# Digits of sorted positions moved from VectorE to GpSimd, and their squares from GpSimd to ScalarE, in a fused attention and mixture-of-experts kernel

## The chip, the cores and the metric

The kernel runs on one core of a Trainium2 chip. A core has five engines that run their own instruction streams in order and meet at semaphores: TensorE (PE in the profile), VectorE (DVE), ScalarE (ACT), GpSimd (POOL) and SyncE (SP, which here only starts DMAs). The metric is the time on the device in microseconds (us); the kernel before takes 2859.86 us, the median of three runs.

## What is computed

Images are cut into 36 patches of 16 x 16 and embedded to 192 numbers each, 77 text tokens are appended, and the 16 x 113 = 1808 tokens go through one attention layer and then through a feed-forward part with a shared expert and 16 gated experts. The gated experts are what matters here. For each token `x` (192 numbers) and each expert `i`:

```
gate_feature = hidden_states * pe[i] @ gate_w + gate_b      # 192 numbers
gate_weight, gate_idx = top_k(gate_feature, 96)             # sorted, with positions
gate_weight = softmax(gate_weight)
gathered = take_along_axis(hidden_states, gate_idx, axis=-1)
y = y + (silu((gathered * gate_weight) @ eg_w[i]) * ((gathered * gate_weight) @ eu_w[i])) @ ed_w[i]
```

So every token needs, for every expert, the 96 largest of 192 gate features in order, their positions, and the token's own numbers at those positions. The positions run from 0 to 191. The softmax subtracts the largest value, which is the first of the sorted ones.

## The kernel before, in words

**Tiles and blocks.** Behind the attention part (the first 335 us or so) the 1808 tokens are worked in 14 tiles of 128 tokens and one rest of 16 tokens, which is packed into one tile's width. A tile's 16 experts are four groups of four; one group of one tile is a block. The rest is block 0 (two packed bands in place of four experts), and the tiles are blocks 1 to 56. `slot(t, g, mlp)` is what each engine does for group `g` of tile `t`; the loop over `t` is unrolled by four groups.

**The search, on VectorE (`slot`, lines 850 to 885).** For each block VectorE handles two pairs of experts. Per pair there are 12 rounds; a round finds the 8 largest (`max`, L867), their positions (`max_index`, L871) and strikes them out (`match_replace`, L873) for both experts of the pair. After the first round of the next block `close_block` (L837) closes the block before: it writes the negated maxima `ntop` (L842) and splits the 384 positions of the block into a high digit (position / 16, L846) and a low digit (position mod 16, L847), both as 16-bit integers in `digits`, and raises `ranked`. VectorE runs ahead of the other engines: for block n it waits only for the gate features of that block and for the softmax weights of block n-2.

**The gather, on the four others.** The gather is made of matmuls. The digits of block n+1 are turned to bf16 by ScalarE (`prepare`, L918) and squared by GpSimd (`square`, L1096); digits and squares (`dcode`) go by DMA to HBM and back into `rows`, laid out anew. In the slot of block n each engine goes through 16 steps (octs, `o` = 0 to 15). Per oct TensorE builds a one-hot code (`make_code`, L1190), ScalarE takes it out of PSUM (`code_out`, L935), TensorE looks the tokens up with it (`look`, L1205), ScalarE takes the result out (L946), GpSimd multiplies it with the second half of the code (`picked`, L1110), and TensorE places the product (`put`, L1214). TensorE builds the code of oct o+2 while it looks up oct o, and has only one PSUM buffer for it: code o+2 waits until ScalarE has taken out code o+1. Between the octs stand the experts' matmuls of the block before (`up` L1252, `down` L1269), ScalarE's `activate` and GpSimd's `hide` for them, and the gate matmuls of the next tile (L1171).

**Where the two halves meet.** `PREPARE` is 8: behind oct 8 of the slot of block n, ScalarE does `prepare(n + 1)`, for which it waits for `ranked`, and GpSimd does `square(n + 1)` behind its `picked` of oct 8, for which it waits for ScalarE's `plain`. Everything on these two engines that is written behind these points waits with them, the four `exponentials` of block n+1 (octs 9 to 12) and all the code and look work of octs 9 to 15 included.

Of the kernel before, what the change touches and what calls it, by code (L numbers as in the profile page):

```python
# [25 lines left out]
TOP = D // 2  # L26
# [548 lines left out]
PREPARE = 8  # L575

# [23 lines left out]
def experts(nc, sb, sem, tok_d, norm_d, normt_d, digit_d, out, ident, wgate, gatew, pe_col, rows, table, wshared, wsdown, wexp, wdown,  # L600
# [11 lines left out]
    digits = sb("digits", [TILE, 2, 2, COLS], U16)  # L612
# [39 lines left out]
    plain = sem("plain")  # L652
# [21 lines left out]
    def steady(eng):  # L674

        eng.sem_inc(passed, 1)
# [67 lines left out]
    with nc.Block() as block:  # L744
# [79 lines left out]
        def _(dve):  # L824
# [12 lines left out]
            def close_block(n, par):  # L837

                many = experts_of(n)
                last = 1 if many > 2 else 0  # L840
                dve.wait_ge(chains[last], LAST_STEP)
                nc.vector.tensor_scalar(ntop[:, par, 0:many], vals[:, par, 0:many, 0], -1.0, None, ALU.mult)  # L842
                if not (isinstance(n, int) and n < 2):
                    dve.wait_ge(plain, n - 1)
                src = idx[:, par, 0:many].rearrange("p e r -> p (e r)")
                nc.vector.tensor_scalar(digits[:, par, 0, 0:many * TOP], src, 4, None, ALU.logical_shift_right)  # L846
                nc.vector.tensor_scalar(digits[:, par, 1, 0:many * TOP], src, LO - 1, None, ALU.bitwise_and).then_inc(ranked, 1)  # L847
                dve.sem_clear(chains[last])

            def slot(t, g, mlp):  # L850
# [3 lines left out]
                for pair in range(many // 2):  # L854
# [26 lines left out]
                    found.then_inc(chain, 1)  # L881
                    done += 1
                    assert done == LAST_STEP
# [15 lines left out]
        def _(act):  # L899
# [12 lines left out]
            def prepare(n, par):  # L912
                act.wait_ge(ranked, n + 1)

                if not isinstance(n, int) or n >= 2:
                    act.wait_ge(digits_out, 16 * n - 16)
                w = experts_of(n) * TOP
                nc.scalar.activation(dcode[:, par, :, 1, 0:w], digits[:, par, :, 0:w], ACT.Copy).then_inc(plain, 1)  # L918
# [128 lines left out]
        def _(pool):  # L1047
# [44 lines left out]
            def square(n, par):  # L1092

                pool.wait_ge(plain, n + 1)
                w = slice(0, experts_of(n) * TOP)
                nc.gpsimd.tensor_tensor(dcode[:, par, :, 0, w], dcode[:, par, :, 1, w], dcode[:, par, :, 1, w],  # L1096
                                        ALU.mult).then_inc(coded, 1)

            def slot(t, g, mlp):
# [5 lines left out]
                for o in range(OCT):  # L1105
# [6 lines left out]
                    if o == PREPARE and not last_block(n):  # L1112
                        square(n + 1, 1 - par)
# [45 lines left out]
            square(0, 0)  # L1159
# [263 lines left out]
```

## Time and profile before

| | |
|---|---|
| median of three runs | 2859.86 us (2857.23 to 2862.73) |
| the profiled execution | 2860.59 us, of which its span is 2858.9 us |
| busy: DVE | 2572.4 us, 90% of the span |
| busy: PE | 2389.7 us, 84% |
| busy: ACT | 1679.0 us, 59% |
| busy: POOL | 1657.0 us, 58% |
| mean granted TensorE clock | 0.929 |

A busy time is the sum of an engine's own instructions; an engine that waits for a semaphore isn't busy. In the row views the last bracket of a row is the idle time of that engine just before the instruction, and what ended it.

### The profile page before, as it was taken

To read this page: it belongs to the slowest core of one execution; us is meant where nothing else is said; L and a number is where in the kernel's file an instruction comes from. 1 tells how busy PE (TensorE), PEld (TensorE's weight loads), DVE (VectorE), ACT (ScalarE), POOL (GpSimd) and SP (SyncE) were. 2 spreads that over 40 slices of the span, in tenths; PEclk is the share of its full clock that TensorE was granted. 3 is DMA by queue.
4 is the path that set the end of the run, shared out by engine and by line. 5 is a ranking of instruction groups with operands and counts; after the bars stand their busy time and mean duration, and the time that the engine had idled before them with its cause. 6 is when DMAs were issued, how large, how long until landed. Compare 5 with 4: busy or idle time off the path is not lost.

```text
span 2858.9 us, 55365 instructions
## 1 busy us (share of the span) xinstructions
PE 2389.7 (84%) x12314; PEld 1572.6 (55%) x12314; DVE 2572.4 (90%) x13628; ACT 1679.0 (59%) x3895; POOL 1657.0 (58%) x2118
## 2 busy tenths in 40 slices
PE   4999649998888887888888888888888888888887
PEld 3677426655555554555555555555555555555554
DVE  2454499999999999999999999999999999999980
ACT  1343233776656666666666656666666666666664
POOL 0110023776766676675666766666676666667675
PEclk9898668999999999999999999999999999999998
DMA  3000410110110111110110110111110110110110
GB/s 97 25 25 24 119 23 14 26 28 15 31 24 17 28 25 21 25 28 16 28 28 14 32 25 16 28 25 21 25 28 16 29 28 14 32 25 15 25 23 5
DMA packets 159240, 77.93 MB, mean 27 GB/s; under 512 B 105911, under 2 KB 156204, under 8 KB 156876
## 3 DMA queue, kind: packets, MB, share of 16 engines
q1 hardware_dynamic: 158156, 72.39, 12.5%
q8 instruction: 127, 2.08, 0.3%
q14 instruction: 253, 2.07, 0.2%
q0 software_dynamic: 704, 1.39, 0.1%
HBM read 39.04 MB, written 27.77 MB: 23 GB/s over the span
## 4 chain that ended last, share of the span: by engine, by line
DVE 85%; PE 2%; issue 1%; ACT 1%; POOL 0%; DMA 0%; POOLq 0%; DVEq 0%; ACTq 0%
DVE idx L871 30%; DVE keys L873 29%; DVE vals L867 24%; DVE digits L847 0%; PE ps L1252 0%; DVE digits L846 0%; PE ps L1214 0%; PE ps L1269 0%; DVE keys_rest L873 0%; PE ps L1190 0%; ACT code L935 0%; DVE ntop L842 0%; PE ps L1205 0%; ACT gu_s L977 0%; PE ps L1181 0%
## 5 line engine op out<-in xcount | busy, mean ns | idle before, releaser
L871 DVE FIND_INDEX8 idx<-vals,keys 128x8 uint16<-128x192 f32 x2688 | 1234.6, 465 | 0.0
L873 DVE MATCH_REPLACE8 keys<-vals,keys 128x192 f32<-128x192 f32 x2464 | 1124.7, 456 | 0.0
L867 DVE MAX8 vals<-keys 128x8 f32<-128x192 f32 x2688 | 973.2, 461 | 0.0
L1110 POOL TENSOR_TENSOR picked<-looked_s,code 128x384 f32<-128x384 f32 (+1 forms) x912 | 810.1, 904 | 76.8 <-ACT looked_s L946 68.1
L935 ACT ACTIVATE code<-ps 128x768 bf16<-128x768 f32 (+1 forms) x912 | 735.6, 807 | 187.2 <-PE ps L1190 168.3
L1190 PE MATMUL ps<-rows,codew 128*128 128x384 bf16 (+1 forms) x1824 | 469.8, 340 | 355.9 <-ACT code L935 326.0
L1214 PE MATMUL ps<-picked,place 128*128 128x384 f32 (+1 forms) x1824 | 753.0, 501 | 0.0
L1205 PE MATMUL ps<-code,table 128*128 128x384 bf16 (+1 forms) x2736 | 615.2, 335 | 29.7 <-issue 29.7
L946 ACT ACTIVATE looked_s<-ps 128x384 f32<-128x384 f32 (+1 forms) x912 | 445.6, 489 | 125.9 <-PE ps L1205 122.9
L871 DVE MATCH_VALUE_LOAD idx<-vals,keys 128x8 f32 x2688 | 512.6, 191 | 0.0
L1190 PEld LDWEIGHTS ps<-rows,codew 128*128 128x128 bf16 x1824 | 150.1, 99 | 575.8 <-ACT code L935 487.7
L873 DVE MATCH_VALUE_LOAD keys<-vals,keys 128x8 f32 x2464 | 456.6, 185 | 0.0
L1205 PEld LDWEIGHTS ps<-code,table 128*128 128x128 bf16 x2736 | 273.9, 101 | 274.2 <-issue 144.4
L1214 PEld LDWEIGHTS ps<-picked,place 128*128 128x128 f32 x1824 | 335.8, 198 | 77.3 <-issue 8.3
L1075 POOL TENSOR_TENSOR prod_s<-gu_s 96x256 f32<-96x256 f32 (+1 forms) x256 | 184.6, 721 | 304.6 <-ACT gu_s L977 301.0
L1252 PEld LDWEIGHTS ps<-xwt,wexp 96*96 96x96 f32 x1792 | 232.8, 171 | 35.2 <-issue 21.3
L1252 PE MATMUL ps<-xwt,wexp 96*96 96x128 f32 x1792 | 246.0, 283 | 1.6 <-ACT gu_s L977 1.0
L1096 POOL TENSOR_TENSOR dcode<-dcode 128x768 bf16<-128x768 bf16 (+1 forms) x57 | 82.9, 1454 | 264.7 <-ACT dcode L918 264.7
L918 ACT ACTIVATE dcode<-digits 128x768 bf16<-128x768 uint16 (+1 forms) x57 | 47.7, 837 | 281.2 <-DVE digits L847 281.2
L976 ACT ACTIVATE tanh_s<-ps 96x256 f32<-96x256 f32 x254 | 95.7, 377 | 193.5 <-PE ps L1252 152.2
L1269 PEld LDWEIGHTS ps<-wdown,hid 96*128 96x128 f32 (+1 forms) x960 | 165.4, 185 | 67.1 <-POOL hid L1079 7.2
L1269 PE MATMUL ps<-wdown,hid 96*128 96x192 f32 (+1 forms) x960 | 195.7, 328 | 2.8 <-POOL hid L1079 2.8
(139 smaller groups left out, 2557.9 us busy)
## 6 DMA issues: line engine op xcount, KB each, us to landing
digit_d<-dcode SPq DMA_DIRECT2D x56, 384.0 KB, 2.6
rows<-digit_d SPq DMA_DIRECT2D x112, 192.0 KB, 4.7
table<-parts SPq DMA_DIRECT2D x240, 9.0 KB
rows<-fill SPq DMA_DIRECT2D x1, 3072.0 KB
wexp<-in_w_exp SPq DMA_DIRECT2D x1, 2304.0 KB
wdown<-in_w_down SPq DMA_DIRECT2D x1, 2304.0 KB
hr<-norm_d SPq DMA_DIRECT2D x120, 12.0 KB
patch<-in_patches SPq DMA_DIRECT2D x16, 108.0 KB, 2.0
```

Source lines behind the costliest of these rows:

```text
L867: nc.vector.max(vals[:, par, e, at], from_keys[:, e, :]).then_inc(chain, 1)
L871: found = nc.vector.max_index(idx[:, par, e, at], vals[:, par, e, at], from_keys[:, e, :])
L873: nc.vector.match_replace(from_keys[:, e, :], vals[:, par, e, at], from_keys[:, e, :], NEG).then_inc(chain, 1)
L935: nc.scalar.activation(code[:, o % 4, :, 0:w], ps[:, CODE_B:CODE_B + 2, 0:w], ACT.Relu).then_inc(code_ready, 1)
L946: nc.scalar.activation(looked_s[:, o % 4, 0:w], ps[:, LOOK_B + o % 2, 0:w], ACT.Copy).then_inc(looked_out, 1)
L1075: nc.gpsimd.tensor_tensor(prod_s[:, u % 2, :, w], gu_s[:, u % 2, 0, :, w], gu_s[:, u % 2, 1, :, w], ALU.mult).then_inc(half_hidden, 1)
L1110: nc.gpsimd.tensor_tensor(picked[:, o % 4, w], looked_s[:, o % 4, w], code[:, o % 4, 1, w], ALU.mult).then_inc(picked_ready, 1)
L1190: ins = nc.tensor.matmul(ps[:, CODE_B + a, w], codew[:, a, :], rows[:, par, o, w], start=True, stop=True)
L1205: ins = nc.tensor.matmul(ps[:, LOOK_B + o % 2, w], table[:, o, s, :], code[:, o % 4, 0, w], start=(s == 0), stop=(s == 2))
L1214: nc.tensor.matmul(ps[:, XG_B, w], place[:, OCT - 1 - o:OCT - 1 - o + TILE], picked[:, o % 4, w], start=(o == 0), stop=(o == OCT - 1)).the ...
L1252: ins = nc.tensor.matmul(dst, wexp[:, e, at:at + HALF], xwt[:, e % GRP, :], start=True, stop=True)
L1269: ins = nc.tensor.matmul(ps[0:REST if rest else TILE, Y_B, 0:D], hid[:, u % 2, c, own], w, start=(u == 0 and c == 0), stop=(u == last_u an ...
```

## The change

VectorE no longer closes a block with three instructions. The last `max_index` of a block raises `ranked` by itself, and `close_block` only waits for the chain semaphore and clears it. GpSimd gets `part_ranks` in the place of `square`: behind `picked` of oct 8 it waits for `ranked` and for the digits' DMA of two blocks before, then writes `ntop`, and makes the digits in fp32. `rough` is position - 7.5 plus a large constant (1.5 x 2^27), at whose size fp32 has steps of 16, so that the sum is rounded to a multiple of 16; `whole` is the position as fp32; `high` is `rough` less the constant; the high digit is that over 16, and the low digit is `whole` less `high`. Both digits are written to `dcode` as bf16, and `parted` is raised. ScalarE's `prepare` waits for `parted` in place of `ranked` and squares the digits (`Square`) in place of copying them, and raises `coded` for the DMA. The semaphore `plain` and VectorE's wait for it are gone; `snapped` orders the steps within `part_ranks`.

```diff
--- before.py
+++ after.py
@@ -573,6 +573,7 @@
 TURN = 2
 DOWN_LAG = 3
 PREPARE = 8
+SNAP = 1.5 * 2.0 ** 27
 
 REST_LIST = [(0, None, 0), (1, None, 1), (2, "band", 0), (3, "band", 1)]
 assert len(REST_LIST) == REST_UNITS
@@ -609,7 +610,9 @@
     keys_rest = sb("keys_rest", [TILE, BANDS, D])
     vals = sb("vals", [TILE, 2, GRP, TOP])
     idx = sb("idx", [TILE, 2, GRP, TOP], U16)
-    digits = sb("digits", [TILE, 2, 2, COLS], U16)
+    rough = sb("rough", [TILE, COLS])
+    whole = sb("whole", [TILE, COLS])
+    high = sb("high", [TILE, COLS])
     dcode = sb("dcode", [TILE, 2, 2, 2, COLS], BF16)
     codew = sb("codew", [128, 2, 128], BF16)
     code = sb("code", [TILE, 4, 2, COLS], BF16)
@@ -649,7 +652,7 @@
     b_ones, b_codew = sem("b_ones"), sem("b_codew")
     gated, keys_ready = sem("gated"), sem("keys_ready")
     chains = sem("chain_first"), sem("chain_second")
-    plain = sem("plain")
+    parted, snapped = sem("parted"), sem("snapped")
     ranked, coded, digits_out, rows_in = sem("ranked"), sem("coded"), sem("digits_out"), sem("rows_in")
     inverted = sem("inverted")
     weights_ready = sem("weights_ready")
@@ -838,13 +841,7 @@
 
                 many = experts_of(n)
                 last = 1 if many > 2 else 0
-                dve.wait_ge(chains[last], LAST_STEP)
-                nc.vector.tensor_scalar(ntop[:, par, 0:many], vals[:, par, 0:many, 0], -1.0, None, ALU.mult)
-                if not (isinstance(n, int) and n < 2):
-                    dve.wait_ge(plain, n - 1)
-                src = idx[:, par, 0:many].rearrange("p e r -> p (e r)")
-                nc.vector.tensor_scalar(digits[:, par, 0, 0:many * TOP], src, 4, None, ALU.logical_shift_right)
-                nc.vector.tensor_scalar(digits[:, par, 1, 0:many * TOP], src, LO - 1, None, ALU.bitwise_and).then_inc(ranked, 1)
+                dve.wait_ge(chains[last], LAST_STEP - 1)
                 dve.sem_clear(chains[last])
 
             def slot(t, g, mlp):
@@ -878,9 +875,11 @@
                             close_pair(0)
                         if r == 0 and pair == 0 and not (isinstance(n, int) and n < 2):
                             close_block(n - 1, 1 - par)
-                    found.then_inc(chain, 1)
-                    done += 1
-                    assert done == LAST_STEP
+                    assert done == LAST_STEP - 1
+                    if pair == many // 2 - 1:
+                        found.then_inc(ranked, 1)
+                    else:
+                        found.then_inc(chain, 1)
                 if last_block(n) or is_rest(t):
                     close_block(n, par)
 
@@ -910,12 +909,12 @@
                                      ACT.Copy).then_inc(xwt_ready, 1)
 
             def prepare(n, par):
-                act.wait_ge(ranked, n + 1)
+                act.wait_ge(parted, n + 1)
 
                 if not isinstance(n, int) or n >= 2:
                     act.wait_ge(digits_out, 16 * n - 16)
                 w = experts_of(n) * TOP
-                nc.scalar.activation(dcode[:, par, :, 1, 0:w], digits[:, par, :, 0:w], ACT.Copy).then_inc(plain, 1)
+                nc.scalar.activation(dcode[:, par, :, 0, 0:w], dcode[:, par, :, 1, 0:w], ACT.Square).then_inc(coded, 1)
 
             def exponentials(n, par, e):
 
@@ -1089,12 +1088,24 @@
                         bass.AP(tensor=p_ap.tensor, offset=p_ap.offset, ap=[list(p_ap.ap[0]), [1, EXPERTS], [0, REST]]),
                         ALU.mult).then_inc(packed, 1)
 
-            def square(n, par):
-
-                pool.wait_ge(plain, n + 1)
-                w = slice(0, experts_of(n) * TOP)
-                nc.gpsimd.tensor_tensor(dcode[:, par, :, 0, w], dcode[:, par, :, 1, w], dcode[:, par, :, 1, w],
-                                        ALU.mult).then_inc(coded, 1)
+            def part_ranks(n, par):
+
+                many = experts_of(n)
+                pool.wait_ge(ranked, n + 1)
+                if not isinstance(n, int) or n >= 2:
+                    pool.wait_ge(digits_out, 16 * n - 16)
+                steady(pool)
+                src = idx[:, par, 0:many].rearrange("p e r -> p (e r)")
+                w = slice(0, many * TOP)
+                nc.gpsimd.tensor_scalar(ntop[:, par, 0:many], vals[:, par, 0:many, 0], -1.0, 0.0, ALU.mult, ALU.add)
+                nc.gpsimd.tensor_scalar(rough[:, w], src, 0.5 - LO / 2, SNAP, ALU.add, ALU.add).then_inc(snapped, 1)
+                nc.gpsimd.tensor_scalar(whole[:, w], src, 1.0, 0.0, ALU.mult, ALU.add).then_inc(snapped, 1)
+                pool.wait_ge(snapped, 4 * n + 1)
+                steady(pool)
+                nc.gpsimd.tensor_scalar(high[:, w], rough[:, w], SNAP, 0.0, ALU.subtract, ALU.add).then_inc(snapped, 1)
+                nc.gpsimd.tensor_scalar(dcode[:, par, 0, 1, w], rough[:, w], SNAP, 1.0 / LO, ALU.subtract, ALU.mult).then_inc(snapped, 1)
+                pool.wait_ge(snapped, 4 * n + 4)
+                nc.gpsimd.tensor_tensor(dcode[:, par, 1, 1, w], whole[:, w], high[:, w], ALU.subtract).then_inc(parted, 1)
 
             def slot(t, g, mlp):
                 n, par = block_no(t, g), parity(t, g)
@@ -1110,7 +1121,7 @@
                     nc.gpsimd.tensor_tensor(picked[:, o % 4, w], looked_s[:, o % 4, w], code[:, o % 4, 1, w],
                                             ALU.mult).then_inc(picked_ready, 1)
                     if o == PREPARE and not last_block(n):
-                        square(n + 1, 1 - par)
+                        part_ranks(n + 1, 1 - par)
                     for (u, e, half), spot in zip(units, spots):
                         if spot == o:
                             hide(tm, u, e)
@@ -1156,7 +1167,7 @@
             pack()
             for step in range(4):
                 split_part(0, step)
-            square(0, 0)
+            part_ranks(0, 0)
             slots(pool, slot)
             for u, e, half in units_of(BPT - 1):
                 hide(TILES, u, e)
```

VectorE, the end of the first full block and the first round of the next, before (`chain_second` is the second pair's semaphore, ISA the semaphore's clearing):

```order
L871 MAX_INDEX idx<-vals,keys 128x8 [waits chain_first]
L873 MATCH_REPLACE keys<-vals,keys 128x192
L871 MAX_INDEX idx<-vals,keys 128x8 [waits chain_first]
L873 MATCH_REPLACE keys<-vals,keys 128x192
L842 TENSOR_SCALAR ntop<-vals 128x4 [waits chain_second]
L846 TENSOR_SCALAR digits<-idx 128x384
L847 TENSOR_SCALAR digits<-idx 128x384
L848 ISA
L867 MAX vals<-keys 128x8 [waits chain_first] x2
```

and in the changed kernel:

```order
L868 MAX_INDEX idx<-vals,keys 128x8 [waits chain_first]
L870 MATCH_REPLACE keys<-vals,keys 128x192
L868 MAX_INDEX idx<-vals,keys 128x8 [waits chain_first]
L870 MATCH_REPLACE keys<-vals,keys 128x192
L845 ISA [waits chain_second]
L864 MAX vals<-keys 128x8 [waits chain_first] x2
```

Three instructions between the first round's last `match_replace` and the next round's `max` are gone; the clearing stays.

GpSimd, in the tiles' loop around oct 8 of one slot (split of the token table, then `picked`, then the prepare step), before:

```order
L1066 TENSOR_TENSOR parts<-rest,parts 96x16x16 [waits rounded]
L1106 REGISTER_ALU
L1110 TENSOR_TENSOR picked<-looked_s,code 128x384 [waits placed,looked_out]
L1094 REGISTER_ALU
L1096 TENSOR_TENSOR dcode<-dcode 128x2x384 [waits plain]
L1106 REGISTER_ALU
L1110 TENSOR_TENSOR picked<-looked_s,code 128x384 [waits placed,looked_out]
L1071 REGISTER_ALU
```

and in the changed kernel:

```order
L1117 REGISTER_ALU
L1121 TENSOR_TENSOR picked<-looked_s,code 128x384 [waits placed,looked_out]
L1094 REGISTER_ALU
L1096 ISA [waits ranked]
L1100 TENSOR_SCALAR ntop<-vals 128x4 [waits digits_out]
L1101 TENSOR_SCALAR rough<-idx 128x384
L1102 TENSOR_SCALAR whole<-idx 128x384
L1103 ISA
L1105 TENSOR_SCALAR high<-rough 128x384 [waits snapped]
L1106 TENSOR_SCALAR dcode<-rough 128x384
L1107 REGISTER_ALU
L1108 TENSOR_TENSOR dcode<-whole,high 128x384 [waits snapped]
L1117 REGISTER_ALU
L1121 TENSOR_TENSOR picked<-looked_s,code 128x384 [waits placed,looked_out]
```

In the place of one instruction that waited for `plain` there are six, of which the first waits for `ranked`, and two wait for GpSimd's own results. ScalarE's order is as it was, with the wait for `parted` in the place of that for `ranked`, and SyncE's order is the same.

## Rows read from the trace of the kernel before

**Rows 1.** The page's chain that ended last, shares of the span by engine.
```profile
DVE 85%; PE 2%; issue 1%; ACT 1%; POOL 0%; DMA 0%; POOLq 0%; DVEq 0%; ACTq 0%
```

**Rows 2.** Timeline, closing of one block: start us, us, engine, line, operation, tiles [idle].
```profile
2041.47 0.47 DVE L871 FIND_INDEX8 idx<-vals,keys 128x8 uint16<-128x192 f32 x1
...
2043.30 0.47 DVE L873 MATCH_REPLACE8 keys<-vals,keys 128x192 f32<-128x192 f32 x1
2043.56 0.28 DVE L842 TENSOR_SCALAR ntop<-vals 128x4 f32<-128x4 f32 x1
...
2043.96 0.74 DVE L867 MAX8 vals<-keys 128x8 f32<-128x192 f32 x2
2044.29 0.84 ACT L918 ACTIVATE dcode<-digits 128x768 bf16<-128x768 uint16 x1 [4.21 <-DVE digits L847]
```

**Rows 3.** Timeline, the closings of blocks 9 and 49, and GpSimd beside one.
```profile
753.20 0.67 POOL L1066 TENSOR_TENSOR parts<-rest,parts 96x256 bf16<-96x256 f32 x1
...
753.27 0.62 DVE L842 TENSOR_SCALAR ntop<-vals 128x4 f32<-128x4 f32 x1
...
754.86 0.61 DVE L867 MAX8 vals<-keys 128x8 f32<-128x192 f32 x2
...
2473.33 0.62 DVE L842 TENSOR_SCALAR ntop<-vals 128x4 f32<-128x4 f32 x1
...
2474.93 0.61 DVE L867 MAX8 vals<-keys 128x8 f32<-128x192 f32 x2
```

**Rows 4.** Timeline, ScalarE and GpSimd at the prepare steps of blocks 2, 3, 56.
```profile
452.68 0.84 ACT L918 ACTIVATE dcode<-digits 128x768 bf16<-128x768 uint16 x1 [13.18 <-DVE digits L847]
...
509.72 0.84 ACT L918 ACTIVATE dcode<-digits 128x768 bf16<-128x768 uint16 x1
...
511.02 1.46 POOL L1096 TENSOR_TENSOR dcode<-dcode 128x768 bf16<-128x768 bf16 x1
...
2773.12 0.47 DVE L871 FIND_INDEX8 idx<-vals,keys 128x8 uint16<-128x192 f32 x1
...
2774.16 0.84 ACT L918 ACTIVATE dcode<-digits 128x768 bf16<-128x768 uint16 x1 [4.21 <-DVE digits L847]
```

**Rows 5.** Groups by line, GpSimd, 512 to 2776 us: xcount | busy, mean ns | idle before.
```profile
L1096 POOL TENSOR_TENSOR dcode<-dcode 128x768 bf16<-128x768 bf16 x54 | 79.1, 1466 | 206.4 <-ACT dcode L918 206.4
```

**Rows 6.** Timeline, one prepare step in a slot with a long wait.
```profile
1313.72 0.84 ACT L918 ACTIVATE dcode<-digits 128x768 bf16<-128x768 uint16 x1 [8.42 <-DVE digits L847]
...
1314.64 1.47 POOL L1096 TENSOR_TENSOR dcode<-dcode 128x768 bf16<-128x768 bf16 x1 [7.68 <-ACT dcode L918]
```

**Rows 7.** Groups by line and form, GpSimd, whole span.
```profile
L1110 POOL TENSOR_TENSOR picked<-looked_s,code 128x384 f32<-128x384 f32 x896 | 801.4, 910 | 58.4 <-ACT looked_s L946 56.1
...
L1063 POOL CAST parts<-rest 96x256 bf16<-96x256 f32 x15 | 6.2, 416 | 0.2 <-POOL rest L1059 0.2
...
L313 POOL COPY hkept<-h 113x192 f32<-113x192 f32 x16 | 5.5, 345 | 1.2 <-DVE xn L401 1.2
L1135 POOL TENSOR_SCALAR st<-st 128x1 f32<-128x1 f32 x15 | 2.9, 190 | 1.9 <-ACT ysq L1003 0.8
```

**Rows 8.** Waits: who waited for whom, us in total, times, longest.
```profile
ACT code L935 <- POOL picked L1110: 11.2, 15, 0.8
...
PEld ps L1269 <- POOL hid L1079: 7.2, 17, 1.8
```

**Rows 9.** Timeline, ScalarE's wait and TensorE's beside it, a short wait.
```profile
1227.77 0.84 ACT L918 ACTIVATE dcode<-digits 128x768 bf16<-128x768 uint16 x1 [2.34 <-DVE digits L847]
...
1229.75 0.50 PE L1190 MATMUL ps<-rows,codew 128*128 128x384 bf16 x2 [0.17 <-ACT code L935]
```

**Rows 10.** Windows: busy us (x) of PE, PEld, DVE, ACT, POOL, then PEclk, DMA.
```profile
1312.00:1319.00 7.00, 3.30 (x10) 1.78 (x11) 7.00 (x41) 4.65 (x12) 4.20 (x5) 0.53 0.18 59
```

**Rows 11.** Groups by line, ScalarE, whole span.
```profile
L1003 ACT ACTIVATE ysq<-y,st 128x192 f32<-128x192 f32 x15 | 6.8, 455 | 9.5 <-POOL st L1131 9.5
...
L320 ACT ACT_TABLE_LOAD x1 | 1.3, 1283 | 0.9 <-PEq L1413 0.9
```

## The prediction, on record before the changed kernel ran

> **What bounds the kernel now.** Read the chain that ended last first: 85% of the span is VectorE [rows 1], and in the expert part VectorE never idles, since every row of a block's closing starts on the heels of the one before [rows 2]. Then ask who waits for VectorE. ScalarE does at the prepare step (2.3 to 13.2 us in the rows shown, [rows 2, 4, 6, 9]), and GpSimd, which stands behind ScalarE there, waits 206.4 us in 53 blocks, 3.89 us a block [rows 5]. So the gathering half has room, but only 3.89 us of 43, and the question of this change is whether what is put onto GpSimd still fits in it. That is read from two pitches.
>
> VectorE's pitch: the closing of block 39 starts at 2043.56 and that of block 49 at 2473.33 [rows 2, 3], which is 42.98 us a block.
>
> The gather's own pitch, if VectorE were never late: from block 3's ScalarE step (509.72) to block 56's (2774.16) there are 53 blocks in 2264.44 us [rows 4]. Less the 206.4 us that GpSimd waited, 2058.0 remain, 38.83 a block. That runs from GpSimd's square to its arrival at the next prepare step. ScalarE starts its own step 0.92 us before that square (1313.72 against 1314.64, [rows 6]), so from ScalarE's resuming to GpSimd's next arrival it is 39.75 us. GpSimd arrives later than ScalarE: at block 3 nobody waited for VectorE, ScalarE was there at 509.72 and GpSimd at 511.02, behind its `picked` of oct 8 [rows 4]. In row pair 6 the same gap is 8.42 + 0.92 - 7.68 = 1.66.
>
> **The change part by part.** *VectorE.* The three instructions that go cost less than their own durations (0.28 us for `ntop` alone), because they overlap: from `ntop` to the next `max` it is 2043.96 - 2043.56 = 0.40 us [rows 2]. 55 full closings lie inside the stream: 22.0 us (block 0's short one is left out). Twice the same stretch took 754.86 - 753.27 = 1.59 and 2474.93 - 2473.33 = 1.60 us [rows 3], 2.4 us more together, each time with GpSimd at work at the start. Together 24.4 us, and VectorE's pitch becomes 42.98 - 0.40 = 42.58. The semaphore's clearing stays; it stood beside the searches and costs nothing as long as they are issued ahead.
>
> On those two slow closings: `ntop` started 0.07 us after a GpSimd instruction. The Trainium skill, "SBUF — State Buffer", section "Who interferes with whom", says that a VectorE tensor_scalar can take the second port pair, which GpSimd shares, and that whoever is first keeps it for the whole instruction. The trace agrees, with these 1.2 us; by that rule they end with the change, and the searches, which run at 0.26 us steps whatever GpSimd does, don't feel GpSimd's added work.
>
> *GpSimd.* Away goes the square of 768 elements, 1.466 us a block [rows 5]. It stood behind ScalarE, so nothing but the digits' DMA and GpSimd's next `picked` waited for it. In come six instructions. A tensor_scalar of one element costs 0.190 [rows 7], so `ntop` 0.19. The trace has no long tensor_scalar on GpSimd. The nearest are the other one-input operations: a copy of 192 elements 0.345, a cast of 256 0.416 [rows 7]. Over the 0.190 that is 0.81 to 0.89 ns an element; 384 elements give 0.50 to 0.53. From above the bound is the two-input product of 384 elements, 0.910 [rows 7]; from below 0.345, the copy of half the size. I take 0.50, nearest to the one-input rows. Four of them 2.0; the last, with two inputs, 0.90; 0.08 us each for the wait on its own results and for the handing over to ScalarE (as 1314.64 follows 1313.72 + 0.84, [rows 6]): 0.19 + 2.0 + 0.90 + 0.16 = 3.25 us a block. With the bounds it is 2.6 and 4.9.
>
> The skill's "GPSIMD Engine Reference", section 4.1 "Engine selection", says that GpSimd is about twice as slow as VectorE with two inputs and roughly at line rate with one. By that rule the four cost 0.5 each and the sum is the same; it speaks against the upper bound.
>
> *ScalarE.* The square of 768 bf16 elements takes the place of a copy of the same size, 0.84 [rows 2]: nothing. Squares run already on ScalarE without a second table load [rows 11]; were one needed at each, it would be 2 x 1.3 us a block.
>
> *The new wait.* Before, ScalarE's step needed only VectorE, and GpSimd squared beside ScalarE's next octs. Now ScalarE stands from its arrival until GpSimd has arrived and worked 3.25 us. Behind it on ScalarE are the looks' and codes' evictions of octs 9 to 15; TensorE can't build code 12 before code 11 is taken out, so it stops too. The gather's pitch becomes 39.75 + 3.25 = 43.00 us, against VectorE's 42.58: the gather is now the slower half. As VectorE isn't held back, all of it shows at the end.
>
> **The sum.** Block 2's step still waits for VectorE (13.18 us before, [rows 4]). Its start moves by: 3.25 us behind the last `max_index`'s end in place of 2044.29 - (2041.47 + 0.47) = 2.35 [rows 2], +0.9; two closings less, -0.7: +0.2. GpSimd comes to block 3 at 511.02 + 0.2 = 511.2, ScalarE resumes at 514.5. Block 56: 514.5 + 53 x 43.00 = 2793.5, against 2774.16: +19.3 us. From there on the tail is as before. Off goes what GpSimd's relief gives: it is free when ScalarE resumes, where before it was busy until 2.39 us after. All that anyone waited for it in those places was 11.2 and 7.2 us [rows 8]; between 0 and 18.4 I take 5. So +14.3 us on the profiled 2860.6: 2874.9. The median of the runs lies 0.7 below the profiled execution: 2874.
>
> **The rivals.**
> (A) VectorE stays the bound, and the change is faster. Mechanism: TensorE works ahead while ScalarE stands, so that a stall isn't paid in full. For it: a stall of 2.34 us of ScalarE left TensorE idle for only 0.17 us [rows 9]. Against it: 39.75 was measured between a resuming behind such a stall and the next arrival, so what TensorE had done ahead is in it already. Time: -24.4, and at the end +2.7, since the last step starts 3.25 us behind the last search's end and not at 2774.16 - (2773.12 + 0.47) = 0.57 [rows 4]: -21.7, 2838. It decides fully where a block's stall adds under 2.6 us in place of 3.25; at 2.98 the time is that of before.
> (B) GpSimd's fp32 tensor_scalar on 16-bit positions runs at the two-input rate, 0.91. Then 4 x 0.41 = 1.64 more in each of 54 steps: 88.6 us, 2963. For it: two arithmetic steps and a conversion in each. Against: the casts convert at 0.416 for 256.
> (C) No change: both effects cancel. It is the strip between the forecast and A, a stall of 2.9 to 3.1 us.
> A further cost in either direction is TensorE's clock. The window behind and around the end of a long stall shows a granted clock of 0.53 of full speed [rows 10], that is mostly the lower of its two levels, 1.2 in place of 2.4 GHz. The new stalls are shorter than the longest of before but come in every slot; I leave it at nothing, give or take 10 us.
>
> **Chances and range.** The forecast, gather-bound at one-input rates, 0.55, with its own range 2850 to 2900 (0.45 to 0.60 us for an instruction moves it by -11 and +22, the relief by +5 and -13). A in whole or part 0.25, of which 0.03 ends within the strip. B or something between it and the forecast 0.20. What a measurement of this kernel can tell from no change is 0.2%, 5.7 us. Faster: 0.22 + 0.01 = 0.23; same: 0.03 + 0.09 = 0.12; slower: 0.45 + 0.20 = 0.65. The range leaves a tenth out on each side: from 2843, within A, to 2950, short of B's end.
>
> **What would show it.** In the profile after: GpSimd's four long tensor_scalars near 0.50 us; `max` following the first round's last `match_replace` at 0.26; almost no idle time of GpSimd before `ntop` from block 3 on, ScalarE idle some 4 to 5 us before its square and waiting for GpSimd, not for VectorE; squares at a pitch of 43.0; and VectorE done with the last block at about 2749, some 40 us before GpSimd comes for it. If GpSimd still waits for `max_index` at most prepare steps and the last one follows VectorE at once, A holds. If the tensor_scalars read 0.8 or more, B.

## The result, and the profile of the changed kernel

The changed kernel takes 3082.0 us, median of 4 runs (3081.7 to 3085.5); the kernel before, on the same chip, 2858.6 (2857.0 to 2862.7). The ratio is 1.078, 95% interval 1.076 to 1.080: 223 us slower. The forecast was 2874, its range ended at 2950. The sign was right, the size was not.

The page of the changed kernel (span 3080.0 us): busy times, the granted clock in 40 slices, and the chain that ended last.
```profile
PE 2433.7 (79%) x12314; PEld 1590.7 (52%) x12314; DVE 2551.3 (83%) x13457; ACT 1684.1 (55%) x3895; POOL 1930.3 (63%) x2403
...
PEclk9999578998898999988999999989889899899998
...
PE 33%; POOL 26%; issue 17%; ACT 8%; DVE 3%; POOLq 1%; ACTq 1%; DMA 0%; DVEq 0%
```
VectorE held 85% of the chain [rows 1] and now holds 3%. The chain runs round the gather's loop, with GpSimd at 26%. So the bound did change sides, as forecast. Then the waits: who, line, for whom; us in total, times, longest.
```profile
ACT dcode L917 <- POOL dcode L1108: 492.8, 57, 23.8
...
DVE vals L864 <- issue: 210.6, 40, 9.0
...
PE ps L1201 <- ACT code L934: 504.5, 197, 24.3
```
ScalarE waits for GpSimd's last digit in all 57 blocks, TensorE behind it for the next code. The same two waits in the kernel before:
```profile
PE ps L1190 <- ACT code L935: 326.0, 213, 23.1
...
ACT dcode L918 <- DVE digits L847: 281.2, 54, 22.6
```
There ScalarE waited for VectorE. How long one such wait is, and what fills it, is in the timelines of ScalarE and GpSimd at one prepare step (start us, us, ..., [idle before]), against [rows 6]:
```profile
1303.58 0.91 POOL L1121 TENSOR_TENSOR picked<-looked_s,code 128x384 f32<-128x384 f32 x1
1304.57 0.20 POOL L1100 TENSOR_SCALAR ntop<-vals 128x4 f32<-128x4 f32 x1
1304.83 1.52 POOL L1101 TENSOR_SCALAR rough<-idx 128x384 f32<-128x384 uint16 x1
1306.43 0.51 POOL L1102 TENSOR_SCALAR whole<-idx 128x384 f32<-128x384 uint16 x1
1307.02 1.50 POOL L1105 TENSOR_SCALAR high<-rough 128x384 f32<-128x384 f32 x1
1308.60 1.50 POOL L1106 TENSOR_SCALAR dcode<-rough 128x384 bf16<-128x384 f32 x1
1310.18 0.99 POOL L1108 TENSOR_TENSOR dcode<-whole,high 128x384 bf16<-128x384 f32 x1
```
```profile
1311.29 0.84 ACT L917 ACTIVATE dcode<-dcode 128x768 bf16<-128x768 bf16 x1 [7.78 <-POOL dcode L1108]
```
From `ntop` to the square (1304.57 to 1311.29) it is 6.72 us where 3.25 were forecast. One of the four long tensor_scalars took the forecast 0.5 us, three took 1.5. GpSimd itself did not wait: it starts `ntop` 0.08 us behind its `picked`. The groups by form show the same for all 56 full blocks (xcount | busy us, mean ns | idle before):
```profile
L1101 POOL TENSOR_SCALAR rough<-idx 128x384 f32<-128x384 uint16 x56 | 84.6, 1512 | 3.5
L1106 POOL TENSOR_SCALAR dcode<-rough 128x384 bf16<-128x384 f32 x56 | 84.0, 1501 | 4.4
L1105 POOL TENSOR_SCALAR high<-rough 128x384 f32<-128x384 f32 x56 | 84.0, 1500 | 4.4
L1108 POOL TENSOR_TENSOR dcode<-whole,high 128x384 bf16<-128x384 f32 x56 | 55.7, 995 | 4.7
L1102 POOL TENSOR_SCALAR whole<-idx 128x384 f32<-128x384 uint16 x56 | 28.6, 511 | 4.4
```
And ScalarE's steps of blocks 3 and 56, against [rows 4]:
```profile
514.03 0.84 ACT L917 ACTIVATE dcode<-dcode 128x768 bf16<-128x768 bf16 x1 [7.82 <-POOL dcode L1108]
...
2995.07 0.84 ACT L917 ACTIVATE dcode<-dcode 128x768 bf16<-128x768 bf16 x1 [7.69 <-POOL dcode L1108]
```
(2995.07 - 514.03) / 53 = 46.81 us a block, forecast 43.00. 3080.0 - 2995.07 = 84.9 us remain behind, as before (2858.9 - 2774.16 = 84.7).

### The profile page after: what moved, and what is told of

It reads as the page before. It is cut to its first block, busy times and chain, and to the rows that moved or that the text cites. A ratio compares the mean times of both kernels' runs of the same rounds, so it can differ in the third digit from the quotient of the medians.

```text
span 3080.0 us, 55737 instructions
## 1 busy us (share of the span) xinstructions
PE 2433.7 (79%) x12314; PEld 1590.7 (52%) x12314; DVE 2551.3 (83%) x13457; ACT 1684.1 (55%) x3895; POOL 1930.3 (63%) x2403
## 4 chain that ended last, share of the span: by engine, by line
PE 33%; POOL 26%; issue 17%; ACT 8%; DVE 3%; POOLq 1%; ACTq 1%; DMA 0%; DVEq 0%
PE ps L1225 10%; POOL picked L1121 8%; PE ps L1201 6%; PE ps L1216 6%; ACT code L934 4%; PE ps L1263 4%; PE ps L1280 3%; POOL rough L1101 3%; POOL dcode L1106 3%; POOL high L1105 3%; POOL turned_s L1076 2%; POOL prod_s L1074 2%; PE ps L1182 2%; POOL dcode L1108 2%; ACT looked_s L945 2%
## 5 line engine op out<-in xcount | busy, mean ns | idle before, releaser
L864 DVE MAX8 vals<-keys 128x8 f32<-128x192 f32 x2688 | 818.9, 346 | 211.0 <-issue 210.6
L868 DVE FIND_INDEX8 idx<-vals,keys 128x8 uint16<-128x192 f32 x2688 | 940.1, 351 | 0.0
L1201 PE MATMUL ps<-rows,codew 128*128 128x384 bf16 (+1 forms) x1824 | 485.1, 350 | 533.0 <-ACT code L934 504.5
L870 DVE MATCH_REPLACE8 keys<-vals,keys 128x192 f32<-128x192 f32 x2464 | 841.6, 342 | 0.0
L1225 PE MATMUL ps<-picked,place 128*128 128x384 f32 (+1 forms) x1824 | 773.2, 512 | 0.0
L1216 PE MATMUL ps<-code,table 128*128 128x384 bf16 (+1 forms) x2736 | 632.5, 342 | 30.6 <-issue 30.6
L917 ACT ACTIVATE dcode<-dcode 128x768 bf16<-128x768 bf16 (+1 forms) x57 | 47.7, 837 | 492.8 <-POOL dcode L1108 492.8
L868 DVE MATCH_VALUE_LOAD idx<-vals,keys 128x8 f32 x2688 | 203.4, 76 | 0.0
L1076 POOL TENSOR_TENSOR turned_s<-prod_s,tanh_s 96x256 f32<-96x256 f32 (+1 forms) x256 | 184.3, 720 | 20.1
L1078 POOL TENSOR_TENSOR hid<-prod_s,turned_s 96x256 f32<-96x256 f32 (+1 forms) x256 | 184.2, 720 | 20.1
```

The costliest lines, as they stand in the source:

```text
L864: nc.vector.max(vals[:, par, e, at], from_keys[:, e, :]).then_inc(chain, 1)
L868: found = nc.vector.max_index(idx[:, par, e, at], vals[:, par, e, at], from_keys[:, e, :])
L870: nc.vector.match_replace(from_keys[:, e, :], vals[:, par, e, at], from_keys[:, e, :], NEG).then_inc(chain, 1)
L1201: ins = nc.tensor.matmul(ps[:, CODE_B + a, w], codew[:, a, :], rows[:, par, o, w], start=True, stop=True)
L1216: ins = nc.tensor.matmul(ps[:, LOOK_B + o % 2, w], table[:, o, s, :], code[:, o % 4, 0, w], start=(s == 0), stop=(s == 2))
L1225: nc.tensor.matmul(ps[:, XG_B, w], place[:, OCT - 1 - o:OCT - 1 - o + TILE], picked[:, o % 4, w], start=(o == 0), stop=(o == OCT - 1)).the ...
```

## The experiments

Below, the stall is the mean time from the start of GpSimd's `ntop` to ScalarE's square over blocks 3 to 56. The own part, the gather loop's time without that stall, is the pitch of the squares (the mean time from one block's square to the next one's) less the stall and less any idle time of GpSimd before `ntop`. Both come from one profiled execution of each kernel.

**What decides 0.5 or 1.5 us.** The three slow instructions differ from the quick one in their pair of operations, in constants (SNAP is 2.0e8), and in part in operand types, and all ran beside VectorE. The kernel before, with twelve forms on 384 elements in GpSimd's idle first microseconds, twice each:
```
+ nc.gpsimd.tensor_scalar(m_out[:], m_pos[:], 1.0, 0.0, ALU.mult, ALU.add).then_inc(micro, 1)
...
+ nc.gpsimd.tensor_scalar(m_out[:], m_pos[:], -7.5, SNAP, ALU.add, ALU.add).then_inc(micro, 1)
...
```


> The kernel before, with twelve tensor_scalars of 384 elements put twice into GpSimd's idle start, while VectorE waits for its weights, each ordered behind the one before. Theory 1, the pair of operations decides: (mult, add) takes 0.51 us on 16-bit and on fp32 input and with the large constant as well, (add, add) and (subtract, mult) take 1.50 whatever the constants. Theory 2, rounding at the large constant is slow: (mult, add) with the large constant takes 1.50, (add, add) with small constants 0.51. Theory 3, GpSimd was slowed by VectorE's searches beside it: all take 0.51 here, where VectorE is idle. The time of the kernel stays at 2859, since GpSimd waits for the weights there anyway.

GpSimd's timeline of that kernel. By line: L311 and L313 (mult, add), L315 (mult, add SNAP), L317 (add, add SNAP), L319 (add, add) with small constants, L321 (subtract, mult), L323 (mult, mult), L325 mult alone, L327 add alone, L329 (not shown) mult alone on positions, L331 (max, add), L333 (mult, add) to 16 bits.
```profile
2.89 0.51 POOL L311 TENSOR_SCALAR m_out<-m_pos 128x384 f32<-128x384 uint16 x1
3.49 0.52 POOL L313 TENSOR_SCALAR m_out<-m_flo 128x384 f32<-128x384 f32 x1
4.08 0.51 POOL L315 TENSOR_SCALAR m_out<-m_flo 128x384 f32<-128x384 f32 x1
4.68 1.53 POOL L317 TENSOR_SCALAR m_out<-m_pos 128x384 f32<-128x384 uint16 x1
6.29 1.50 POOL L319 TENSOR_SCALAR m_out<-m_flo 128x384 f32<-128x384 f32 x1
7.87 1.51 POOL L321 TENSOR_SCALAR m_out<-m_flo 128x384 f32<-128x384 f32 x1
9.46 0.52 POOL L323 TENSOR_SCALAR m_out<-m_flo 128x384 f32<-128x384 f32 x1
10.06 1.18 POOL L325 TENSOR_SCALAR m_out<-m_flo 128x384 f32<-128x384 f32 x1
11.32 1.18 POOL L327 TENSOR_SCALAR m_out<-m_flo 128x384 f32<-128x384 f32 x1
...
13.84 1.50 POOL L331 TENSOR_SCALAR m_out<-m_flo 128x384 f32<-128x384 f32 x1
15.43 0.51 POOL L333 TENSOR_SCALAR m_int<-m_pos 128x384 uint16<-128x384 uint16 x1
```
m_pos holds 16-bit integers, m_flo fp32. The pair decides. (mult, add) and (mult, mult) take 0.51 us, the other pairs 1.50, one operation alone 1.18. Constants and types change nothing here, and (add, add) takes 1.50 with VectorE idle as it did in the changed kernel beside VectorE's searches. The second pass read the same within 0.03 us. The kernel's time, of a single run, was 2861.1 us (2858.9 without the addition).

**The same six instructions with quick pairs.** The rounding is left out, all else stays.
```
- nc.gpsimd.tensor_scalar(rough[:, w], src, 0.5 - LO / 2, SNAP, ALU.add, ALU.add).then_inc(snapped, 1)
+ nc.gpsimd.tensor_scalar(rough[:, w], src, 1.0, 0.0, ALU.mult, ALU.add).then_inc(snapped, 1)
...
- nc.gpsimd.tensor_scalar(high[:, w], rough[:, w], SNAP, 0.0, ALU.subtract, ALU.add).then_inc(snapped, 1)
- nc.gpsimd.tensor_scalar(dcode[:, par, 0, 1, w], rough[:, w], SNAP, 1.0 / LO, ALU.subtract, ALU.mult).then_inc(snapped, 1)
+ nc.gpsimd.tensor_scalar(high[:, w], rough[:, w], 1.0, 0.0, ALU.mult, ALU.add).then_inc(snapped, 1)
+ nc.gpsimd.tensor_scalar(dcode[:, par, 0, 1, w], rough[:, w], 1.0 / LO, 0.0, ALU.mult, ALU.add).then_inc(snapped, 1)
```


> The changed kernel with the three slow pairs written as mult and add with 1.0 or 1/16 and 0.0: the same six instructions and waits, but the rounding is left out, so the digits are not the right ones. If the pair decides and the gather's pitch is 40.1 us plus ScalarE's stall, the stall falls by 3 x 0.99 from 6.72 to 3.75, the pitch from 46.8 to 43.8, and the time by 54 x 2.97 = 160 us to 2922. If the stalls were partly hidden beside TensorE's work, it falls by less than 160. If the pair doesn't decide, it stays at 3082.

2930.6 us (ratio 1.023, 1.020 to 1.027), where 2922 was expected. Writing three instructions with another pair takes away 151 of the 223 us. The stall fell from 6.71 to 3.40: 3.0 us are the three instructions, the other 0.3 shorter gaps between the six (the quick ones start 0.47 to 0.59 us apart; in the change each started 0.08 us behind the end of the one before). The pitch fell by less, 46.81 to 43.97, because the own part rose from 40.08 to 40.55.

**Seven quick instructions that compute the change's digits**, the first addition split in two:
```
+ nc.gpsimd.tensor_scalar(centred[:, w], src, 1.0, 0.5 - LO / 2, ALU.mult, ALU.add).then_inc(snapped, 1)
...
+ nc.gpsimd.tensor_scalar(rough[:, w], centred[:, w], 1.0, SNAP, ALU.mult, ALU.add).then_inc(snapped, 1)
...
+ nc.gpsimd.tensor_scalar(high[:, w], rough[:, w], 1.0, -SNAP, ALU.mult, ALU.add).then_inc(snapped, 1)
...
+ nc.gpsimd.tensor_scalar(dcode[:, par, 0, 1, w], high[:, w], 1.0 / LO, 0.0, ALU.mult, ALU.add).then_inc(snapped, 1)
```


> The changed kernel with every step as mult and add, which needs one more instruction (position - 7.5, then plus the large constant) and one more wait, and gives the right digits. Stall 3.75 + 0.51 + 0.1 = 4.35 us, pitch 44.4, time 3082 - 54 x 2.37 = 2954. If large constants make it slow, two of the five stay at 1.50 and the time is 3060.

2946.1 us (1.030, 1.029 to 1.032) at a stall of 4.54, where 2954 and 4.35 were expected.

**Two instructions**, `ntop` and the two digit columns written straight from the positions, with the rounding and the subtraction left out, and the same with two more that write `rough` and `whole`:
```
+ nc.gpsimd.tensor_scalar(dcode[:, par, 0, 1, w], src, 1.0 / LO, 0.0, ALU.mult, ALU.add)
+ nc.gpsimd.tensor_scalar(dcode[:, par, 1, 1, w], src, 1.0, 0.0, ALU.mult, ALU.add).then_inc(parted, 1)
```


> The changed kernel with only the negated maxima and two mult and add instructions on GpSimd, each digit straight from the position, without rounding (so the digits are wrong). Stall 1.4 us, the gather's pitch 41.5, below VectorE's 42.58: VectorE bounds, and its whole saving shows: 2859 - 24.4 + 0.8 = 2836 (last step 1.4 behind the last search in place of 0.57). If VectorE's saving were smaller than 0.40 us a block, or the gather's own pitch without its waits higher than 40.1 + 1.4, it is above 2840.

> The changed kernel with ntop and four tensor_scalars of the pair mult and add, no rounding and no subtraction, so the digits are wrong. Stall from GpSimd's start to ScalarE's: 0.28 + 4 x 0.59 + about 0.07 = 2.7 us. Theory (the larger of two pitches: VectorE's 42.6, and 39.75 plus the stall): 39.75 + 2.7 = 42.45, still under VectorE's, so 2832 to 2840 us, as with two instructions (2832) although the stall is 1.2 us longer. Rival 1 (every microsecond of stall counts, since the clock and the tails follow it): 2832 + 53 x 1.2 = 2896. Rival 2 (the own pitch is 40.5 when all six instructions are mult and add, as that run showed, so the two pitches meet earlier): 40.5 + 2.7 = 43.2, 53 x 0.6 = 32 us more, 2864.

With two 2831.9 us (0.991, 0.989 to 0.993), with four 2848.0 (0.997, 0.996 to 0.998). At a stall of 1.45 `ntop` waits for VectorE and the searches close at a pitch of 42.56 us; at 2.60 it no longer waits, and the squares' pitch is 42.43, near the 39.75 + 2.60 = 42.35 that the forecast's own part gives. The two pitches meet there. With four it took 16 us more than with two, 8 above the theory's band and as far, 16 us, below rival 2. That rival's reason, an own part of 40.5, did not hold here: it was 39.81. Rival 1 (2896) is out.

**The square alone on ScalarE**, digits and maxima left on VectorE, whose wait for `plain` becomes one for `coded`:
```
  nc.scalar.activation(dcode[:, par, :, 1, 0:w], digits[:, par, :, 0:w], ACT.Copy)
+ nc.scalar.activation(dcode[:, par, :, 0, 0:w], digits[:, par, :, 0:w], ACT.Square).then_inc(coded, 1)
...
- square(n + 1, 1 - par)
```


> The kernel before with one part of the change alone: the squares go from GpSimd (one tensor_tensor of 1466 ns per block) to ScalarE (one Square of about 0.84 us per block, as in the changed kernel, behind the Copy). VectorE keeps the digits and the maxima, so its pitch of about 42.7 us stays. Theory (the stall of ScalarE behind GpSimd's chain is the whole loss; GpSimd's freed 1.47 us and ScalarE's 0.84 us are worth nothing while VectorE closes last): 2859 us, within 4 of the kernel before; ScalarE goes on 0.84 us later per block, and the gather's own pitch would be 39.8 + 0.8 = 40.6 us, two us under VectorE's. Rival 1 (the Square on ScalarE is a cost of its own on the path): 53 x 0.84 = 45 us, 2904. Rival 2 (GpSimd's queue was a limit and its relief counts): under 2850.

2863.3 us (1.002, 1.001 to 1.003), 4.8 more than before, just past the 4 that were allowed. That part of the change is nearly free, and both rivals are out: 45 us for the square are not there, nor a gain. VectorE's closing (`ntop` to the next `max`, 0.40 us in [rows 2]) was longer than 0.45 us in 17 blocks in place of 4, and in these the excess over 0.40 adds up to 7.9 us in place of 3.0. Each time a GpSimd instruction was under way when `ntop` started. These sums vary from one execution to the next: in the kernel with the twelve forms, whose loop is that of before, it was 7 blocks and 4.6 us. So the delay is seen, but that it is the whole of the 4.8 us is not shown. One such closing, timeline of both engines:
```profile
576.72 1.78 POOL L1103 TENSOR_TENSOR picked<-looked_s,code 128x384 f32<-128x384 f32 x2
...
578.06 0.46 DVE L841 TENSOR_SCALAR ntop<-vals 128x4 f32<-128x4 f32 x1
578.43 0.51 DVE L845 TENSOR_SCALAR digits<-idx 128x384 uint16<-128x384 uint16 x1
...
578.80 0.92 POOL L1103 TENSOR_TENSOR picked<-looked_s,code 128x384 f32<-128x384 f32 x1
578.87 0.96 DVE L846 TENSOR_SCALAR digits<-idx 128x384 uint16<-128x384 uint16 x1
579.76 0.35 DVE L866 MAX8 vals<-keys 128x8 f32<-128x192 f32 x1
```
The second digit starts 0.07 us behind a `picked`, takes 0.96 us where the mean of its line in this kernel is 0.262, and ends 0.11 us behind it. The Trainium skill, "SBUF — State Buffer", section "Who interferes with whom", describes such a lock, in which whoever issues first holds the port pair that VectorE and GpSimd share. This trace agrees, with 1.70 us for this closing.

**Rounding by a 16-bit output**, all on GpSimd, four quick tensor_scalars and the subtraction (`hidig` is a tile of 16-bit integers):
```
+ nc.gpsimd.tensor_scalar(hidig[:, w], src, 1.0 / LO, 0.5 / LO - 0.5, ALU.mult, ALU.add).then_inc(snapped, 1)
...
+ nc.gpsimd.tensor_scalar(high[:, w], hidig[:, w], float(LO), 0.0, ALU.mult, ALU.add).then_inc(snapped, 1)
+ nc.gpsimd.tensor_scalar(dcode[:, par, 0, 1, w], hidig[:, w], 1.0, 0.0, ALU.mult, ALU.add)
```


> The changed kernel's arithmetic on GpSimd with the rounding done by an unsigned 16 bit output instead of the large constant: ntop, four tensor_scalars of the pair mult and add at 0.51 us and one tensor_tensor of 1.0 us, no pair at 1.5 us. Stall: 0.28 + 4 x 0.59 + 1.0 + 0.1 = 3.75 us instead of 6.71. Theory: pitch 39.75 + 3.75 = 43.5 us, 514 + 53 x 43.5 + 84.9 = 2904.4 of span, 2906 us (2890 to 2925 by what the granted clock did in the two runs with six and seven mult and add instructions). Rival (the slow three are not the whole of the loss): above 2960.

2943.6 us (1.030, 1.028 to 1.032) at a stall of 3.61. That is 38 us above the 2906 expected and 19 above its range, although the stall was even shorter than the 3.75 expected. The own part was 40.5 us, as in the kernel with six quick instructions, where the one with seven had 39.7. Next, one and two more instructions in this chain:
```
+ nc.gpsimd.tensor_scalar(extra0[:, w], src, 1.0, 0.0, ALU.mult, ALU.add)
```


> The kernel with the rounded output and one more tensor_scalar of 0.51 us (positions copied to a tile that nobody reads) in GpSimd's chain: stall 3.61 + 0.59 = 4.20 us. The question is why the gather's own part (pitch less stall) was 40.5 us at stalls of 3.4 and 3.6, where the lower level of TensorE's clock took 6.05 and 5.86 us a block, and 39.7 at 4.54, where it took 4.64. Theory (the length of the stall decides at what point the clock falls and comes back, so the own part falls as the stall grows from 3.6 to 4.5): own 39.7 to 40.2, pitch 43.9 to 44.4, 2937 to 2955 us. Rival (the own part hangs on something else in that kernel, such as its five waits of GpSimd on its own results; each microsecond of stall costs one): 40.5 + 4.2 = 44.7, 2943.6 + 53 x 0.59 = 2975 us.

> The same with two more tensor_scalars of 0.51 us: stall 3.61 + 1.18 = 4.79 us. Theory (the stall's length sets the clock's part, which was at its smallest at 4.54): own 39.7, pitch 44.5, 2958 us (2950 to 2970), the lower level of the clock 4.5 to 5 us a block. Rival (the own part stays at 40.5): pitch 45.3, 2943.6 + 53 x 1.18 = 3006 us, the lower level near 5.9 us a block.

2938.7 us (1.028, 1.026 to 1.030) and 2964.9 (1.036, 1.034 to 1.039), both within the theory's bands. The stalls grew by 0.48 and 0.49 us, not by 0.59 each; the first step cost nothing, the second 26 us. All kernels that keep the change's order and differ only in GpSimd's chain, from their profiled executions, sorted by stall; PEclk is the granted clock from 520 to 2700 us (before: 0.96, pitch 42.73):

| kernel | stall | own part | pitch | PEclk | median us |
|---|---|---|---|---|---|
| two | 1.45 | VectorE bounds | 42.25 | 0.97 | 2831.9 |
| four | 2.60 | 39.81 | 42.43 | 0.96 | 2848.0 |
| six quick | 3.40 | 40.55 | 43.97 | 0.93 | 2930.6 |
| rounded output | 3.61 | 40.52 | 44.15 | 0.93 | 2943.6 |
| one more | 4.09 | 40.05 | 44.16 | 0.93 | 2938.7 |
| seven quick | 4.54 | 39.72 | 44.28 | 0.95 | 2946.1 |
| two more | 4.58 | 40.00 | 44.60 | 0.94 | 2964.9 |
| the change | 6.71 | 40.08 | 46.81 | 0.91 | 3082.0 |

The windows behind that column, six quick and seven quick (us, busy of PE, PEld, DVE, ACT, POOL with counts, PEclk):
```profile
520.00:2700.00 2180.00, 1853.95 (x9169) 1193.40 (x9168) 2112.00 (x11501) 1380.71 (x2960) 1500.28 (x2004) 0.93 0.12 23
```
```profile
520.00:2700.00 2180.00, 1809.29 (x9121) 1169.68 (x9120) 2100.41 (x11437) 1366.96 (x2944) 1521.31 (x2040) 0.95 0.12 23
```
At 0.93 a matmul takes 1853.95 / 9169 = 202 ns, at 0.95 198: between these two the longer own part goes with more time at the lower of the clock's two levels, 1.2 GHz. From 3.61 to 4.09 us of stall the own part shrank by half a microsecond, so the rival of a fixed own part (2975 and 3006) is out. But the theory that put this down to the clock is not borne out either. Rounded output and one more, from block 3's square to block 56's:
```profile
509.94:2849.87 2339.93, 1975.90 (x9824) 1271.41 (x9824) 2237.47 (x12177) 1478.02 (x3167) 1613.38 (x2149) 0.93 0.12 23
```
```profile
510.36:2850.91 2340.55, 1973.58 (x9824) 1268.63 (x9824) 2235.50 (x12171) 1477.47 (x3166) 1638.73 (x2202) 0.93 0.12 23
```
The clock is the same, 0.9336 in four digits, which is 5.86 us a block at the lower level in both (twice 1 - 0.9336, times the pitch), and so is TensorE's matmul time (2.3 us apart in 53 blocks); the own part differs by 0.47 us a block all the same. With two more, 5.7 us a block were at the lower level (0.9365), where the theory wanted 4.5 to 5. Two kernels with nearly the same stall (4.54 and 4.58) differ by 0.28 us a block, and the change has the lowest clock without the longest own part. So neither the stall's length nor the time at the lower level alone sets the own part, and the cause of its 0.8 us spread stays open. Wrong digits are not it: six quick has them and rounded output has not, at the same own part.

**The split shared by ScalarE and GpSimd**, looking for a better version:
```
+ nc.scalar.activation(hidig[:, 0:w], src, ACT.Copy, scale=1.0 / LO, bias=0.5 / LO - 0.5).then_inc(stepped, 1)
+ nc.scalar.activation(whole[:, 0:w], src, ACT.Copy).then_inc(raised, 1)
...
+ nc.scalar.activation(high[:, 0:w], hidig[:, 0:w], ACT.Copy, scale=float(LO)).then_inc(raised, 1)
+ nc.scalar.activation(dcode[:, par, 0, 1, 0:w], hidig[:, 0:w], ACT.Copy).then_inc(stepped, 1)
...
+ act.wait_ge(parted, n + 1)
...
+ pool.wait_ge(raised, 2 * n + 2)
  nc.gpsimd.tensor_tensor(dcode[:, par, 1, 1, w], whole[:, w], high[:, w], ALU.subtract).then_inc(parted, 1)
```


> The split shared by two engines: ScalarE rounds the high digit (Copy with scale and bias to an unsigned 16 bit output), copies the positions to fp32, scales the high digit and writes it out, 4 activations of about 0.45 us each; GpSimd does only the negated maxima and one tensor_tensor for the low digit (1.0 us); the squares are on ScalarE. Theory: ScalarE comes to the block some 2 us before GpSimd in the changed kernel (it waited 8.6 us for a chain of 6.7), so its three first copies are done when GpSimd comes; stall 0.28 + 1.0 + 0.1 = 1.4 us, own pitch 41.2, VectorE closes last at 42.6: 2832 to 2842 us, faster than both. Rival (the four activations stand on the path too: stall 1.6 + 1.1 + 0.1 = 2.8 or more, own pitch 42.6 to 43.3 us): 2840 to 2880.

2833.2 us (0.991, 0.990 to 0.993), 25 us faster than before and 249 than the change, inside the expected 2832 to 2842; nothing of the computation is left out. A prepare step of it, ScalarE and GpSimd:
```profile
1295.39 0.52 ACT L918 ACTIVATE hidig<-idx 128x384 uint16<-128x384 uint16 x1 [3.67 <-DVE idx L868]
1295.55 0.20 POOL L1108 TENSOR_SCALAR ntop<-vals 128x4 f32<-128x4 f32 x1 [2.16 <-DVE idx L868]
1295.82 0.51 ACT L919 ACTIVATE whole<-idx 128x384 f32<-128x384 uint16 x1
...
1296.23 0.51 ACT L921 ACTIVATE high<-hidig 128x384 f32<-128x384 uint16 x1
...
1296.64 0.51 ACT L922 ACTIVATE dcode<-hidig 128x384 bf16<-128x384 uint16 x1
...
1296.82 0.99 POOL L1110 TENSOR_TENSOR dcode<-whole,high 128x384 bf16<-128x384 f32 x1 [1.07 <-ACT high L921]
...
1297.90 0.84 ACT L925 ACTIVATE dcode<-dcode 128x768 bf16<-128x768 bf16 x1 [0.76 <-POOL dcode L1110]
```
Both engines wait for VectorE again: it is the bound, and its digits are gone from it. The stall in this block is 2.35 us and not the 1.4 expected, since ScalarE came no earlier than GpSimd, which then waited 1.07 us for `high`. With the searches closing at a pitch of 42.57 us that costs nothing.

## Why the prediction was wrong, by its steps

**What bounds: right.** The gather's own part was worked out as 39.75 us; measured 40.08 under the change, 39.72 to 40.55 over all kernels. Block 3's step was put at 514.5 and came at 514.03. The tail stayed.

**VectorE's saving: right.** 42.98 - 0.40 = 42.58 us was forecast; where VectorE bounds or nearly so (two, four, shared) the searches close at 42.56 to 42.57. With two instructions the kernel is 27 us faster; rival A's 24.4, less 2.7 at the end, has the right mechanism and is 5 us short. Its threshold of 2.6 us of stall is where the pitches met.

**GpSimd's instructions: this step failed.** The price of four long tensor_scalars was taken as 0.50 us from a copy and a cast [rows 7], and for the range the two-input 0.91 was taken as an upper bound. Three of the four took 1.50, and the six instructions with their gaps 6.71 us in place of 3.25. The mistake was to price an instruction by the number of its inputs; a tensor_scalar has two operations, and on this engine their pair sets the rate: 1.50 us for each pair of the change that is not (mult, add), half as much again as the 0.995 of the two-input subtraction. No row of the trace before had a long tensor_scalar, so "from above 0.910" bounded nothing. The Trainium skill's "GPSIMD Engine Reference", section 4.1 "Engine selection", has one input roughly at line rate; the runs agree for (mult, add) at 0.51 and not for (add, add) at 1.50. Rival B looked for the loss in the same instructions, but expected it of the 16-bit positions and at the two-input rate, and stopped at 2963; two of the three slow ones read fp32, and the quick one reads the positions.

**The new wait: right in kind.** ScalarE stood 7.7 to 7.8 us in the rows shown, all of it behind GpSimd, 8.2 on the mean, where 4 to 5 were forecast. The chain was paid for whole: with a stall of 6.71 us what is left of the pitch is 40.08, and not less than the 39.75 worked out without it.

The forecast's span was 2873.2 (2874.9 less the 1.7 of the profiled execution outside it), the measured one 3080.0. The 206.8 us between, in the forecast's terms: stall 6.71 - 3.25 = 3.46 us by 53 blocks, 183.4 (of the 3.46, 3.01 are the three slow instructions, 0.10 the subtraction at 0.995 for 0.90, 0.02 the two that were priced nearly right, and 0.33 the gaps, priced at 0.16 in all and measured at 0.49); own part 0.33 by 53, 17.5; GpSimd's relief, taken as 5 us and not seen, 5: ScalarE's code still waits 10.1 us for `picked`, before 11.2, and the `down` matmuls' weights 7.2 for `hid`, as before [rows 8]; start and tail -0.3. Sum 205.6; the last 1.2 is nearly all the difference between own part plus stall, 46.79, and the pitch of 46.81.

**The own part held at 39.75, with the clock left at nothing, give or take 10: second failure.** Had the stall been 3.25 to 3.4, the time would not have been 2874 but near the 2930.6 measured at 3.40. Of the 57 us between, the stall's excess over 3.25 is 8 and the own part's over 39.75, 0.80 by 53, is 42; the relief that was not seen is 5. How much of the 42 is the clock is open. For it: with four instructions (own part 39.81) the clock was 0.96 and a matmul took 1873.48 / 9499 = 197 ns, with six quick 202, and 5 ns on each of the 185 matmuls of a block are 0.9 us. Against it: rounded output and one more have one and the same clock, 0.93, and differ by 0.47 us a block.

**VectorE done at 2749: wrong, and harmless.** Its last search started at 2957.04. It waits before a block's first `max` until the exponentials of two blocks back are done, so it can't run 40 us ahead for long: these are the 210.6 us above, and in all but one of those waits behind 500 us the `max` starts 0.13 us behind the end of such an exponential. It still came 31 us before `ntop` at 2988.44 needed it.

## What to carry to other kernels

Before work goes to an idle engine, ask who stands behind it: here GpSimd had four tenths of its time free before and the chain was still paid in full, because ScalarE and TensorE stop for it in every block. Price an instruction by its exact operations, and where the trace has none of that kind, measure it; a dozen forms fit into the idle start of a kernel. Write GpSimd's scalar arithmetic as multiply and add where it can be (1.0 us less here for each two-operation instruction of 384 elements), and divide a chain so that two engines meet in the middle.

## What of the hardware was not expected

- GpSimd, tensor_scalar, 384 elements: (mult, add) and (mult, mult) 0.51 us; (add, add), (subtract, mult), (subtract, add), (max, add) 1.50; one operation 1.18. At 192 elements the pair (subtract, mult) took 0.86 and (mult, add) 0.35.
- GpSimd and ScalarE both round to the nearest integer into a 16-bit output, at no cost in time (0.51 and 0.52 us). The digits of the rounded output and of the shared split rest on it.
- A stall of ScalarE cost up to 0.8 us a block more than its length: most at 3.4 to 3.6 us, hardly at 2.6 or 4.54. TensorE's granted clock goes with it in part (0.93, 0.96 and 0.95), but does not explain it: at 4.09 us the clock is 0.93 too, with 0.47 us less. The cause stays open.
